# Filler matmuls at the start of an attention stage: two small groups removed, one group of 18 put in a step later

## The reference

```python
h_sparse = _sparsify_2to4(silu(x @ w_gate) * (x @ w_up))       # L0 ffn
return h_sparse @ w_down
...
# L1 attention: 8 heads of 8 channels, over 256 feature positions
qk = jnp.einsum('bhdq,bhdl->bhql', qh, kh) * scale
sm = jax.nn.softmax(qk, axis=-1)
ret = jnp.einsum('bhql,bhdl->bhdq', sm, vh)
...
x = x + tanh(g_xattn[0]) * L0_attention(layernorm(x), ctx, ctx)
x = x + tanh(g_ffn[0])   * L0_ffn(layernorm(x))
x = x + tanh(g_xattn[1]) * L1_attention(layernorm(x), ctx, ctx)
x = x + tanh(g_ffn[1])   * L1_ffn(layernorm(x))
```

## Time and profile before

| | us |
|---|---|
| runs of the kernel | 670.67, 671.17, 675.47 |
| median | 671.17 |
| the profiled execution: time | 675.47 |
| the profiled execution: span from first to last instruction | 673.7 |
| time around the span (675.47 - 673.7) | 1.8 |
| mean granted TensorE clock, share of full speed | 0.95 |
| `feed_forward0`, from barrier to barrier | 106.6 to 260.9 |
| `attention1`, from barrier to barrier | 260.9 to 485.9 |

### The profile page before, as it was taken

How to read it: one execution, slowest core, us unless ns; L and a number is a source line. 1 busy time by engine, 2 the same in 40 slices (tenths; PEclk the granted TensorE clock), 3 DMA queues, 4 the chain that set the end, 5 groups by cost and what they waited for, 6 DMA issues and landing times. The chain is left out here.

```text
span 673.7 us, 16760 instructions
## 1 busy us (share of the span) xinstructions
PE 605.9 (90%) x5037; PEld 463.2 (69%) x5037; DVE 493.1 (73%) x999; ACT 404.8 (60%) x829; POOL 312.9 (46%) x430
## 2 busy tenths in 40 slices
PE   3688877999999968899999999999789799999995
PEld 2577765788888867455555555555578699999875
DVE  2877885778878796998989999995555634444756
ACT  3888883344434441688988988998545135555431
POOL 2455555023233556945765765752327334124254
PEclk9999995999999988799999999999969789999998
DMA  5434448400000014444444444440002325446344
GB/s 164 115 99 132 124 111 286 152 1 1 0 0 1 23 48 135 125 133 123 141 138 119 140 138 122 144 137 19 3 0 79 125 94 188 143 151 190 115 135 131
DMA packets 72601, 71.20 MB, mean 106 GB/s; under 512 B 12364, under 2 KB 68812, under 8 KB 72556
## 3 DMA queue, kind: packets, MB, share of 16 engines
q1 hardware_dynamic: 67324, 56.33, 28.2%
q0 software_dynamic: 5232, 14.29, 6.8%
HBM read 38.48 MB, written 31.36 MB: 104 GB/s over the span
## 5 line engine op out<-in xcount | busy, mean ns | idle before, releaser
L1426 DVE TENSOR_REDUCE a_smax<-a_s 128x2 f32<-128x512 f32 x256 | 164.3, 680 | 14.2 <-PE a_s L1354 9.1
L1245 ACT ACTIVATE a_prob<-a_st 128x512 f32<-128x512 f32 x256 | 141.9, 597 | 20.7 <-PE a_st L1344 19.5
L1344 PEld LDWEIGHTS a_st<-qop,kop 64*128 64x128 f32 x512 | 71.4, 188 | 59.9 <-DVE a_smax L1426 26.3
L1344 PE MATMUL a_st<-qop,kop 64*128 64x256 f32 x512 | 105.1, 317 | 2.9 <-DVE a_smax L1426 1.7
L1354 PE MATMUL a_s<-kop,qop 64*128 64x256 f32 x512 | 107.1, 319 | 0.0
L1306 PE MATMUL a_pv<-a_prob,a_vt 128*32 128x256 f32 x1024 | 82.5, 394 | 3.2 <-ACT a_pv_sb L1230 1.7
L823 POOL TENSOR_TENSOR f_hs_lo<-f_kept,f_hs_hi 128x512 fp32r<-128x512 f32 x32 | 41.2, 1319 | 86.7 <-ACT f_hs_hi L773 86.7
L1354 PEld LDWEIGHTS a_s<-kop,qop 64*128 64x128 f32 x512 | 73.4, 191 | 0.0
L1877 POOL DMA_INDIRECT sorted_rows<-m_xn,m_slot x32 | 33.5, 1048 | 48.7 <-PE m_gu L128 28.7
L126 PE MATMUL f_bank<-f_xt_hi,w_hi 128*128 128x512 f32 x128 | 51.6, 403 | 1.2 <-DVE w_raw L869 0.6
L127 PE MATMUL f_bank<-f_xt_lo,w_hi 128*128 128x512 f32 x128 | 51.0, 398 | 0.0
(11 more groups left out here) (267 smaller groups left out, 1685.6 us busy)
## 6 DMA issues: line engine op xcount, KB each, us to landing
qop<-qop_rows SPq DMA_DIRECT2D x64, 100.0 KB
kop<-kop_rows SPq DMA_DIRECT2D x64, 96.0 KB
sorted_rows<-x_all SPq DMA_DIRECT2D x2, 2944.0 KB, 15.4
qop<-sorted_rows SPq DMA_DIRECT2D x46, 128.0 KB, 2.4
expert_rows<-turned SPq DMA_DIRECT2D x46, 128.0 KB
kop_rows<-k_hi SPq DMA_DIRECT2D x32, 128.0 KB, 2.3
qop_rows<-q_hi POOLq DMA_DIRECT2D x30, 128.0 KB, 2.7
x_all<-in_x SPq DMA_DIRECT2D x4, 512.0 KB, 4.8
```

The costliest lines, as they stand in the source:

```text
L1245: act.activation(prob[:, u % 8], st_ps[BANK[u]][:], ACT.Exp, scale=SCALE1).then_inc(prob_ready, 1)
L1344: st = pe.matmul(st_ps[BANK[u]][:, c * D:(c + 1) * D], lhsT=kop[t.slot][rows, u // 2, c * P:(c + 1) * P], rhs=qop[t.slot][rows, u // 2], s ...
L1426: dve.tensor_reduce(smax[:, v.slot, opposite(u)], s_ps[BANK[u]][:].rearrange("p (q n) -> p q n", q=2), AX_X, ALU.max).then_inc(smax_ready, 1)
```

## The change

`AWAKE` and its ten matmuls at the end of `feed_forward0` go, together with the wait before them. The 48 repeated products in step 1 of `attention1` go. In step 2, ahead of the matmuls of u = 4, TensorE issues `keep_active(18)`: 18 matmuls with 512 columns over the whole array, into `pv_ps`, which nothing holds at that time.

```diff
@@ feed_forward0
-        AWAKE = 10
...
             group(LAST)
             down(Step(GROUPS - 1, 0, 1), 1)
-            pe.wait_ge(silu_ready, GROUPS * 8)
-            for i in range(AWAKE):
-                pe.matmul(g_ps[0][:], lhsT=w[0][:, 0, 0, i % 4, 0:P], rhs=xt[0][:, 0], start=True, stop=True)
@@ attention1
+        FILL = 18
         WARM = 10
...
                 for u in range(UNITS):
+                    if t.known and t.n == 0 and u == 4:
+                        keep_active(FILL)
                     if t.inside(TILES):
...
-                        elif v.known and v.n == 0:
-                            rows = slice(u % 2 * WIDE, (u % 2 + 1) * WIDE)
-                            for k in range(1 + c):
-                                pe.matmul(st_ps[BANK[u]][:, c * D:(c + 1) * D], lhsT=kop[v.slot][rows, u // 2, c * P:(c + 1) * P],
-                                          rhs=qop[v.slot][rows, u // 2], start=True, stop=True, tile_position=(u % 2 * WIDE, 0))
```

## The result

The change makes the kernel slightly slower: 675.54 us median (674.0 to 679.92, 10 runs) against 671.12 us (668.44 to 675.47, 10 runs) on the same chip, a ratio of 1.0065 with a 95% interval of 1.0043 to 1.0087. That is 4.4 us, 2.9 to 5.8 us.

What follows compares the result with a forecast made beforehand. TensorE, busy 90% of the span, was taken to set the pace, VectorE only in step 1. Terms of -0.4, +6.5 and -3.5 us summed to +2.6 us, hence 673.8 us against a 671.17 us median; range 670.4 to 676.0 us.

Steps and rivals of the forecast that it cites:

- part 1: End of feed_forward0: without the ten matmuls before the barrier, the next block is released 0.4 us sooner.
- The ten before the barrier: Removing the ten matmuls at the end of feed_forward0 makes VectorE last to arrive; release 0.4 us sooner.
- The 48 in step 1: Removing the filler in step 1 of attention1 costs and gains nothing, as VectorE sets the pace: 0, at most 0.3 us.
- The step stays covered even at half clock: Step 1: at half clock TensorE needs 0.43 us for each u, VectorE 0.61 us, so VectorE hides it.
- gaps of VectorE in step 1: Sign in the profile after: sixteen maxima without gaps were forecast; gaps would show the claim about the 48 wrong.
- part 2: Step 1 of attention1: removing the 48 filler matmuls changes nothing, since VectorE sets the pace; 0 us taken.
- The 18: Step 2, ahead of u = 4: twelve matmuls at half clock, six at full, 6.5 us in all.
- Rival (a): Step 2: clock full or rising early, so the 18 take 4.1 us; about 671.3 us; chance 0.15 together with another rival.
- What they buy back: Step 2 from u = 4 to step 3: 8.97 us at full clock in place of 12.51, so 3.54 us back.
- a blocked negation: Rest of step 2: one negation on VectorE blocked by GpSimd work could add up to 0.7 us.
- Rival (b): Step 2: VectorE and ScalarE hide part of the 18, the negation isn't blocked; faster, 670.1 us; chance 0.07.
- Rival (c): Step 2: the 18 don't lift the clock, or it falls again; 7.4 us later, 678.6 us; chance 0.05.

Runs made afterwards that it cites:

- e5: The change with its 18 matmuls left out, so no filler at all there, against the kernel before: ratio 1.0017 (0.9984 to 1.005).
- e1: The unchanged kernel run again, no edit, against the kernel before: ratio 0.998 (0.9941 to 1.0018).
- e11: The unchanged kernel, a further execution with no edit: 668.76 us.
- e3: Only the 48 filler matmuls of step 1 removed from the kernel before: ratio 1.0002 (0.9972 to 1.0032).
- e4: Only the 18 matmuls in step 2 added to the kernel before, all other filler kept: ratio 1.0059 (1.0027 to 1.009).
- e8: No ten, 48 or 18, but one 512-column matmul on all rows behind each u of step 1, against the kernel before: ratio 1.0108.
- e9: As e8, but each filler matmul on 64 rows in place of 128; against the kernel before: ratio 1.0005 (0.9988 to 1.0023).
- e6: The change with 9 filler matmuls in place of 18, against the kernel before: ratio 1.0009 (0.998 to 1.0038).
- e7: The change with 36 filler matmuls in place of 18, against the kernel before: ratio 1.0087 (1.0056 to 1.0117).

## Why the prediction was right, and where its size was off

The mechanism was right: the 18 start at half clock in the stream of the engine that sets the pace, and the delay reaches the end. The place at which step 3 begins was right too, 291.92 - 260.53 = 31.4 us after the release by the forecast (260.53 being 260.93 less the 0.4 us of part 1) and 31.47 and 31.62 us measured. What it was compared with was not. The sum had four terms.

**The ten before the barrier, forecast -0.4 us.** Shown in every trace without them: VectorE's wait for the release is 0.52 to 0.53 us in place of 0.89 us, -0.36 us.

**The 48 in step 1, forecast 0, with 0.3 us as the upper bound.** Off by a little. With the 18 in place, they start 275.23 - 258.81 = 16.42 us after the release, where u = 4 started 15.9 us after it before: 0.5 us later. At half clock the transposes and score matmuls at the end of step 1 no longer keep ahead of VectorE, which waits 0.33 and 0.29 us. "The step stays covered even at half clock" held for twelve of the sixteen maxima; by the prediction's own sign (gaps of VectorE in step 1) part 2 was wrong, by 0.5 us.

**The 18, forecast 6.5 us.** Measured 6.39 us from their start to u = 4 (275.23 to 281.62); half clock at first, full before their end, as forecast. Rival (a), in which they start at full clock, occurred in no trace.

**What they buy back, forecast -3.5 us.** This is the term that was mis-sized. The rest of step 2 after the change was 290.28 - 281.62 = 8.66 us, near the 8.97 us forecast. But the 12.51 us that it was set against came from one execution. The four traces of the unchanged kernel have 12.51, 9.04, 11.0 and 9.04 us there, on average 10.4 us, so the rest of step 2 is 10.4 - 8.7 = 1.7 us shorter on average, and not 3.5 us. And these 1.7 us are not the work of the 18: e5, which has none, takes 8.98 us there, so that the 18 themselves buy 0.3 us. The text noted that the profiled execution was 4.3 us above the median, and did not ask whether the low clock in step 2 was part of that.

With the measured terms the sum is -0.36 + 0.5 + 6.39 - 1.7 = +4.8 us, within the 2.9 to 5.8 us measured. Four traces are few for an average, and from step 3 to the end of the block the traces scatter by a further 3.3 us (195.6 to 198.9 us; 195.6 and 198.3 us in the two of the change), so the match to a few tenths is not shown, only the direction and the rough size of the term.

That the time lies inside the stated range is in part luck. The mechanism's own bounds were +2.0 to +3.4 us, and 0.7 us more for a blocked negation; the measured +4.4 us lie above them, and the range holds it through the margin left for scatter. The prediction also held that a measurement can tell only about 1% from no change; ten executions of each kernel told 0.65%.

Rival (b), faster, had a true core that pointed the other way: at full clock VectorE sets the pace of step 2, but this was so before the change, in e1 and e11, and it made the filler dearer. Rival (c), in which the clock does not rise, didn't occur. e3 and e5 add what the forecast left out: without the 48 (e3) the ratio is at most 1.0032, and with no filler at this seam at all (e5) at most 1.005, so neither group of filler that the kernel had could be shown to be worth anything.

That a delay in step 2 reaches the end was right: 4.0 us for e4 and 4.4 us for the change, with about 5 us later at step 3.

## What to carry to other kernels

Before a stretch at low clock in one trace is counted as time to be won, look whether other executions have it: here it came and went with the execution, and the term built on it was at least twice too large. Filler in a stream that sets the pace costs its own length; it pays only if it saves more than that, and work that TensorE alone holds up gains at most half of the time that it would spend at half clock. Here the clock rose during that work without filler too (e3, e5). Filler on all rows between real matmuls on 64 rows cost 0.6 us for each u (e8), and the same filler on 64 rows did not (e9), so filler should keep to the row pattern of its neighbours.

## What the runs showed of the hardware

Going between matmuls on 64 rows and matmuls on all 128 rows cost about 0.3 us for each change at half clock (0.72 us for a piece in e8 against 0.42 to 0.43 us in e9). Two matmuls on opposite 64 rows ran side by side (the filler and every second u's scores in e9: 0.64 us a u for work that takes 0.85 us in a row).

The granted clock stayed at half over 20 us in which the trace calls TensorE busy for 20.00 us (e8), and over 18 us with 17.05 us busy (e9). In these two kernels the busy time in the trace was no sign that the clock would rise.

Behind u = 3 of step 2 the clock rose 1.2 us (e6), 2.0 us (e7) and 4.4 us (the change) after the start of the filler, in kernels that are the same up to there. Counted from the release that is 17.6, 18.5 and 20.9 us, and 17.3 us in e5, which has no filler there. So the place of the rise scatters by over 3 us between executions, and the filler did not bring it forward.
